# One row tile first: splitting the load and the norm of x ahead of a cross-attention loop

## The reference

```python
c = layernorm(x);  q = ctx
s = (c @ w_c + b_c)[:, :, None] + (q @ w_q + b_q)[:, None, :] + einsum('bcd,bqd,d->bcq', c, q, w_cq) + b_cq
a = softmax(s, axis=2);  c2q = a @ q
b = softmax(max(s, axis=2), axis=1);  q2c = b @ c
x = x + concat([c, c2q, c * c2q, c * q2c]) @ W_l.T + b_l
e = argmax(layernorm(x) @ wr + br)
x = x + gelu(layernorm(x) @ w1[e] + b1[e]) @ w2[e] + b2[e]
```

## Time and profile before

| | us |
|---|---|
| median of 3 runs | 275.74 |
| lowest, highest | 275.59, 278.57 |
| span of the profiled execution | 277.8 |
| the profiled execution's own time beyond its span | not listed |
| VectorE busy | 191.0 (69%) |
| ScalarE busy | 155.9 (56%) |
| GpSimd busy | 109.8 (40%) |

### The profile page before, as it was taken

The page is one execution under the profiler, slowest core; times in us unless marked ns, Lnnn a source line. Parts: engine busy times, 40 slices in busy tenths (PEclk is TensorE's granted clock), DMA queues, the critical chain, the costliest instruction groups (busy, mean ns, idle before and its releaser), DMA issues.

```text
span 277.8 us, 5155 instructions
## 1 busy us (share of the span) xinstructions
PE 202.6 (73%) x1661; PEld 143.8 (52%) x1662; DVE 191.0 (69%) x404; ACT 155.9 (56%) x244; POOL 109.8 (40%) x88
## 2 busy tenths in 40 slices
PE   0249489799779979899898995899540039788960
PEld 0113136556546756576566664799440029566850
DVE  2996967948967979889799798978643013465360
ACT  3299176695568569599595994891100016445430
POOL 2369991942901603507116069400004600424233
PEclk9999978979959999999999999899855556999797
DMA  6992079969968999999989989498001261111000
GB/s 252 391 347 79 0 229 179 250 135 204 249 165 153 226 236 228 247 226 252 255 211 261 235 198 214 113 227 146 0 0 38 104 182 48 43 29 43 10 22 0
DMA packets 129245, 44.64 MB, mean 161 GB/s; under 512 B 107927, under 2 KB 127023, under 8 KB 129231
## 3 DMA queue, kind: packets, MB, share of 16 engines
q1 hardware_dynamic: 128216, 42.87, 65.0%
q0 software_dynamic: 864, 1.58, 1.7%
q10 hardware_dynamic: 150, 0.00, 0.0%
HBM read 14.15 MB, written 4.01 MB: 65 GB/s over the span
## 4 chain that ended last, share of the span: by engine, by line
PE 40%; DVE 21%; issue 19%; ACT 8%; DMA 6%; POOL 3%; ACTq 1%; DVEq 0%; POOLq 0%
ACT Pf L564 5%; DVE S L702 5%; PE psS L922 5%; PE psO L937 4%; PE psS L923 4%; PE psS L924 4%; PE psX L937 4%; DVE Phl L720 3%; DMA PT<-Phl 3%; POOL rows_by_expert L502 2%; PE psS L1111 2%; PE psO L940 2%; DVE qTl L691 2%; DVE c_sb L666 2%; PE psX L940 2%
## 5 line engine op out<-in xcount | busy, mean ns | idle before, releaser
L702 DVE TENSOR_SCALAR_CACHE_REDUCE S<-psS 128x1024 f32<-128x1024 f32 (+1 forms) x56 | 61.8, 1105 | 23.7 <-PE psS L924 15.2
L564 ACT ACTIVATE Pf<-S,negb 128x1024 f32<-128x1024 f32 (+1 forms) x56 | 59.1, 1055 | 33.6 <-DVE negb L711 33.6
L720 DVE TENSOR_TENSOR Phl<-Pf,Phl 128x1024 f16<-128x1024 f32 x41 | 58.8, 1433 | 1.3 <-ACT Phl L580 1.3
L922 PE MATMUL psS<-qTh,gh 128*128 128x512 f16 (+1 forms) x104 | 42.0, 404 | 22.5 <-DVE S L702 9.3
L580 ACT CAST Phl<-Pf 128x1024 f16<-128x1024 f32 x48 | 50.2, 1046 | 10.1 <-DMA PT<-Phl 8.0
L447 POOL TENSOR_TENSOR Phl<-Pf,Phl 128x1024 f16<-128x1024 f32 x7 | 15.6, 2226 | 75.8 <-ACT Phl L580 75.8
L923 PE MATMUL psS<-qTl,gh 128*128 128x512 f16 (+1 forms) x104 | 41.8, 402 | 0.0
L924 PE MATMUL psS<-qTh,gl 128*128 128x512 f16 (+1 forms) x104 | 41.7, 401 | 0.0
L937 PE MATMUL psO<-qn,PT 128*128 128x256 f16 x204 | 39.7, 287 | 0.0
L940 PE MATMUL psO<-qn,PT 128*128 128x128 f16 x204 | 37.8, 228 | 0.0
L937 PE MATMUL psX<-qn,PT 128*128 128x256 f16 x204 | 37.5, 278 | 0.0
(11 more groups left out here) (182 smaller groups left out, 394.5 us busy)
## 6 DMA issues: line engine op xcount, KB each, us to landing
stageT<-in_w SPq DMA_DIRECT2D x8, 512.0 KB, 4.4
stageT<-in_ctxT SPq DMA_DIRECT2D x6, 512.0 KB, 6.6
PT<-in_ctx SPq DMA_DIRECT2D x6, 512.0 KB, 6.8
rows_by_expert<-stageT SPq DMA_DIRECT2D x5, 385.5 KB, 3.5
S<-rows_by_expert SPq DMA_DIRECT2D x1, 967.5 KB, 5.5
S<-rows_by_expert SPq DMA_DIRECT2D x15, 64.0 KB, 1.8
PT<-Phl SPq DMA_TRANSPOSE x48, 3.9
Pf<-in_x SPq DMA_DIRECT2D x1, 512.0 KB, 4.0
```

Of the source, the lines that this page charges most:

```text
L564: nc.scalar.activation(Pf[:, e % 3, 0:b - a], S[:, a:b], ACT.Exp, bias=negb[:, bass.ds(t, 1)], accum_out=Lp[:, bass.ds(t * NG + e, 1)]).th ...
L702: nc.vector.tensor_scalar(out=S[:, a:b], in0=psS[n % 3][:, 0:b - a], scalar1=1.0 / GS, scalar2=None, op0=ALU.mult, op1=ALU.max, accum_out= ...
L720: nc.vector.tensor_tensor(lo, Pf[:, e % 3, 0:hi.shape[1]], hi, ALU.subtract).then_inc(low_done, 1)
L922: nc.tensor.matmul(dst, g_h, qTh[:, a:b], start=True, stop=False)
```

## The change

x is loaded in two parts, row tile 0 straight into `c_sb`, then behind the first ctxT load the other seven. Row tile 0 is normalised, transposed and split alone; tiles 1 to 3 and 4 to 7 follow (`C_GROUPS`), with their statistics, scales and `c_sb` in different places of VectorE's list: the `c_sb` of tiles 1 to 3 and their g among the readouts of tile 0, those of tiles 4 to 7 after the first `negb`. The pieces whose low part GpSimd makes are 0, 2, 4, each in two halves with a semaphore count for each. ScalarE makes four `qn` casts before the first exponential and the other three between the pieces of tile 0, followed by the two cT copies and the late g behind pieces 4 and 5. `row_terms` moves from step 0 to step 1, and the steps 1 and 6 stand outside the loop. GpSimd's list is otherwise as it was.

```diff
+    EARLY = 4
+        C_GROUPS = ((0, 1), (1, H), (H, T))
-        POOL_LOW = (0, 2, 5)
+        POOL_LOW = (0, 2, 4)
-            sp.dma_start(x_sb[:, :, :], x.rearrange("(t p) d -> p t d", p=P)).then_inc(x_landed, 16)
+            sp.dma_start(c_sb[:, 0, :], x[0:P, :]).then_inc(x_landed, 16)
...
+                if n == 0:
+                    sp.dma_start(c_sb[:, 1:T, :],
+                                 x[P:N, :].rearrange("(t p) d -> p t d", p=P)).then_inc(x_rest_landed, 16)
...
             for n in POOL_LOW:
-                a, b = cols(n, GR)
                 pool.wait_ge(qTh_ready, n + 1)
-                nc.gpsimd.tensor_tensor(qTl[:, a:b], stageT[:, a:b], qTh[:, a:b],
-                                        ALU.subtract).then_inc(qTl_pool_ready, 1)
+                for c in (2 * n, 2 * n + 1):
+                    a, b = cols(c, CH)
+                    nc.gpsimd.tensor_tensor(qTl[:, a:b], stageT[:, a:b], qTh[:, a:b],
+                                            ALU.subtract).then_inc(qTl_pool_ready, 1)
...
-            deviation(1, 0, H)
+            deviation(1, 0, 1)
...
-                    deviation(2, H, T)
+                    deviation(2, 1, T)
...
-            act.wait_ge(cT_in_psum, 2)
-            act.wait_ge(g_ready, 2)
-            for h in range(2):
+            def keep_cT(h):
+                act.wait_ge(cT_in_psum, h + 2)
                 nc.scalar.copy(cT[:, h * CH:(h + 1) * CH], cT_psum[h][:, :]).then_inc(cT_ready, 1)
...
+            for n in range(EARLY):
+                high_qn(n)
...
-            step(0, False)
+            for e in range(NG):
+                exp_piece(0, e)
+                high(0, e, False)
+                if EARLY + e < NG:
+                    high_qn(EARLY + e)
+                elif e == EARLY:
+                    keep_cT(0)
+                elif e == EARLY + 1:
+                    keep_cT(1)
+                    late_g()
...
+            def first_g(k):
+                t0, t1 = C_GROUPS[k]
+                a, b = t0 * P, t1 * P
+                dve.wait_ge(cT_in_psum, k + 1)
+                link(nc.vector.tensor_scalar(g32[:, a:b], cT_psum[0][:, a:b], vecs16[:, 0:1], vecs16[:, 1:2],
+                                             ALU.mult, ALU.add))
+                link(nc.vector.tensor_copy(gh[:, a:b], g32[:, a:b]))
+                nc.vector.tensor_tensor(gl[:, a:b], g32[:, a:b], gh[:, a:b], ALU.subtract).then_inc(g_ready, 1)
...
+            dve.wait_ge(x_landed, 16)
+            statistics(c_sb, 0, 1)
+            normalise(c_sb, c_sb, 0, 1, c_ready)
+            dve.wait_ge(x_rest_landed, 16)
+            moments(c_sb, 1, H)
+            first_g(0)
+            link(moments(c_sb, H, T))
+            for t in range(1, T):
+                last = nc.vector.bn_aggr(out=mv[:, t, :], in_=st[:, t, :])
+            link(last)
+            variances(1, T)
...
+            low_qT(1)
+            scores(0, 0, False)
+            low_qT(3)
+            scores(0, 1, False)
+            scales(1, T)
+            standardise(c_sb, c_sb, 1, H, c_ready)
+            low_qT(5)
+            scores(0, 2, False)
+            low_qT(6)
+            scores(0, 3, False)
+            first_g(1)
+            for n in range(4, NG):
+                scores(0, n, False)
             row_max(0)
+            standardise(c_sb, c_sb, H, T, c_ready)
             step(0, 0, False, True)
-            dve.wait_ge(row_term_in_psum, 1)
-            nc.vector.tensor_copy(row_term[:, :], psX[:, 0:T]).then_inc(row_term_ready, 1)
-            with dve.Fori(1, T - 2, 2) as t:
-                step(t, 1, True, True)
-                step(t + 1, 0, True, True)
+            step(1, 1, True, True)
+            with dve.Fori(2, T - 2, 2) as t:
+                step(t, 0, True, True)
+                step(t + 1, 1, True, True)
+            step(T - 2, 0, True, True)
...
             def step(t, odd, has_prev, has_next):
                 for e in range(NG):
+                    if not has_prev and e == 2:
+                        turn_c(2)
                     if not has_prev and e == LAG:
+                        pe.wait_ge(cT_ready, 1)
+                    if isinstance(t, int) and t == 1 and e == 1:
                         row_terms()
+                    if isinstance(t, int) and t == 1 and e == LAG:
+                        pe.wait_ge(row_term_ready, 1)
...
+            pe.wait_ge(g_ready, 1)
+            for c in range(NCH):
...
+                if c == 5:
+                    turn_c(1)
             pe.wait_ge(g_ready, 2)
```

More of the change, by code:

```diff
@@ L337, in _ @@
             sp.wait_ge(qTl_ready, len(DVE_LOW))
[L338 removed]
+            sp.wait_ge(qTl_pool_ready, 2 * len(POOL_LOW))
             def load_w1(k):
@@ L535, in _, with high_qn @@
                 nc.scalar.copy(qTh[:, a:b], stageT[:, a:b]).then_inc(qTh_ready, 1)
-            for n in range(NG):
+            def high_qn(n):
                 act.wait_ge(qn_landed[n], 16)
@@ L642, in _, with moments, statistics @@
             norms = [0]
-            def statistics(src, t0, t1):
+            def moments(src, t0, t1):
                 for t in range(t0, t1):
                     last = nc.vector.bn_stats(out=st[:, t, :], in_=src[:, t, :])
-                link(last)
+                return last
+            def statistics(src, t0, t1):
+                link(moments(src, t0, t1))
                 for t in range(t0, t1):
@@ L651, in statistics, with variances, scales @@
                 link(last)
-            def normalise(src, dst, t0, t1, done):
+            def variances(t0, t1):
                 r = slice(t0, t1)
                 nc.vector.tensor_scalar(sc2[:, r], mv[:, r, 1], EPS, None, ALU.add).then_inc(var_ready, 1)
+            def scales(t0, t1):
+                r = slice(t0, t1)
                 norms[0] += 1
@@ L664, in normalise, with standardise @@
                 link(nc.vector.tensor_tensor(rstd[:, r], rstd[:, r], sc1[:, r], ALU.mult))
+            def standardise(src, dst, t0, t1, done):
                 for t in range(t0, t1):
@@ L667, in normalise @@
                                             ALU.subtract, ALU.mult).then_inc(done, 1)
-            dve.wait_ge(x_landed, 16)
-            statistics(x_sb, 0, H)
-            normalise(x_sb, c_sb, 0, H, c_ready)
+            def normalise(src, dst, t0, t1, done):
+                variances(t0, t1)
+                scales(t0, t1)
+                standardise(src, dst, t0, t1, done)
+            def first_g(k):
[6 more added lines that the diff above has]
+                nc.vector.tensor_tensor(gl[:, a:b], g32[:, a:b], gh[:, a:b], ALU.subtract).then_inc(g_ready, 1)
             dve.wait_ge(small_landed, 16 * NSMALL)
             nc.vector.tensor_scalar(vecs16[:, :], vecs[:, 0:2], GS, None, ALU.mult).then_inc(vecs16_ready, 1)
+            nc.vector.tensor_copy(b3r[:, :], b3s[:, :].broadcast_to([3, T])).then_inc(b3r_ready, 1)
             dve.wait_ge(vecs16_ready, 1)
[L675 to L682, removed]
-            statistics(x_sb, H, T)
-            normalise(x_sb, c_sb, H, T, c_ready)
+            dve.wait_ge(x_landed, 16)
[9 more added lines that the diff above has]
+            variances(1, T)
             def low_qT(n):
@@ L736, in step @@
                 for e in range(NG):
+                    if isinstance(t, int) and t == 1 and e == 1:
+                        dve.wait_ge(row_term_in_psum, 1)
+                        nc.vector.tensor_copy(row_term[:, :], psX[:, 0:T]).then_inc(row_term_ready, 1)
                     if e == LAG and has_prev:
@@ L899, in _, with turn_c @@
             pe.wait_ge(consts_ready, 3)
-            def turn_c(h):
-                for t in range(h * H, (h + 1) * H):
+            def turn_c(k):
+                for t in range(C_GROUPS[k][0], C_GROUPS[k][1]):
                     pe.wait_ge(c_ready, t + 1)
-                    last = nc.tensor.transpose(cT_psum[h][:, (t - h * H) * P:(t - h * H + 1) * P], c_sb[:, t, :],
+                    last = nc.tensor.transpose(cT_psum[t // H][:, (t % H) * P:(t % H + 1) * P], c_sb[:, t, :],
                                                idf[:, :])
```

44 lines of the change are left out of this document (20 added, 24 removed).

## The result

The changed kernel takes 287.0 us (median of 4, 286.54 to 287.85) where the kernel before takes 275.66 (median of 4, 272.67 to 278.57): ratio 1.0453, 95% interval 1.0365 to 1.054. The change is slower, as forecast. The forecast was 283.6, so the loss on the medians is 11.3 us where 7.9 was worked out; 287.0 lies inside the stated 279 to 289, but above the 281 to 286 of "my own case". On the two traces the loss is 285.1 - 277.8 = 7.3.

What follows compares the result with a forecast made beforehand. No engine is full; waits between engines bound the kernel, through when each row tile gets its softmax offset negb. Terms -2.6 + 9.5 + 1.0 = +7.9 us on the 275.74 median gave 283.6, range 279 to 289.

Steps and rivals of the forecast that it cites:

- (a): Start, loads: row tile 0 lands at 2.6 to 4.8 us, the small vectors at 4.0, the rest of x at 5.8.
- (b): Start, row tile 0 normalised alone: the first score matmul moves from 13.14 to 9.05 us, 4.1 earlier.
- (c): Start, VectorE's next statistics, aggregates and variance end at 10.85 us; the third ctxT cast follows at 11.2.
- (d): VectorE until the first negb: 15.8 us work plus 7.0 waiting for GpSimd, offset 0 near 33.8, 2.6 gained.
- (e): Tile 0, ScalarE: added casts and copies and a later transposing DMA put the late gh 19.7 us after negb.
- (f): Tile 0, GpSimd's unchanged order: low piece (0, 3) follows late gl and constants; seventh exponential 26.7 after negb, 9.5 us lost.
- (g): Step 0, TensorE: its fifth group waits for the first cT copy, 15.9 us after negb, at no cost.
- (h): Step 1, row terms moved in and DMAs queued: 1.0 us lost, ends 2.5 lost and 2 gained.
- (i): Unrolling steps 1 and T-2: costed at nothing, with 1 us allowed if unrolled code had to be fetched.
- Given back: Rival: tiles 1 and 2 return up to 8.2 us of the delay, 272.3 us, faster; 6 in 100.
- Row tile 0 not early: Rival: small vectors or rest of x land late, the start gains nothing, 286.2 us; 10 in 100.
- The start lost too: Rival: GpSimd gets between every two VectorE instructions, offset 0 at 37.6, total 288.4 us; 17 in 100.

Runs made afterwards that it cites:

- e3: The changed kernel with the scales of row tiles 1 to 7 moved directly behind their variance, ahead of GpSimd's third ctxT piece: 287.43 us, ratio 1.0477 to the kernel before.
- e5: e1 plus one wait: GpSimd's seven qn low parts are held until VectorE has made g of row tiles 1 to 3: 277.41 us, ratio 1.0103.
- e1: The changed kernel with GpSimd making low piece (0, 3) ahead of its wait for the late gh: 281.75 us, ratio 1.0256 to the kernel before.
- e2: The kernel before with one added wait: GpSimd waits for the sixth high part of tile 0 ahead of its late gl: 282.28 us, ratio 1.0326.
- e6: e1 with ScalarE copying the first half of cT before its first exponential instead of behind piece 4: 278.18 us, ratio 1.0124 to the kernel before.
- e11: The kernel before, unedited, timed and profiled once more: 277.44 us (272.53 to 278.66, 10 runs), ratio 0.997 to the same kernel.
- e8: The kernel before with GpSimd's route constants first and its qn low parts held until VectorE's last low part of ctxT: 278.15 us, ratio 1.0103.
- e10: e9 with all seven qn casts before ScalarE's first exponential instead of four: 270.28 us, ratio 0.988 to the kernel before.
- e9: e5 and e6 together, route constants at GpSimd's start, and the last four c_sb before GpSimd's held run: 272.58 us, ratio 0.9932 to the kernel before.

## Why the forecast held, and where its size was off

- **(a) Right, early.** Small vectors at 2.96 (forecast 4.0), row tile 0 with them; but the rest of x at 6.92 (5.8), for which VectorE waited 1.48.
- **(b) Right.** First score matmul at 9.39 (9.05) where the earlier trace rows have 13.14. The early landing was spent on the late rest, and on the cast `gh`, 1.07 from 7.94 beside 0.36 for three times its width later on.
- **(c) Right.** The variances end at 10.9; the next low part starts at 10.84.
- **(d) The waits were mis-sized.** From 10.84 to 35.38 are 24.5 us. Waits, by rows: 1.0 in the low part at 13.32, 6.3 in the four scales (6.99 less 4 x 0.17), 1.75 in the three `c_sb` (2.61 less 0.86), 0.5 for TensorE: 9.6, where 7.0 was put; the work was 15.0, where 15.8 was put. The premise "where VectorE's instructions stand back to back it seems to keep its turn" is refuted: by e3's three `c_sb`, 6.28, and e5's four, 7.71. The row at 18.63 was one case, in which GpSimd came out of a wait only 0.06 us before, and was read as a rule. The Trainium skill, "SBUF — State Buffer", section "Who interferes with whom", has the two engines shut each other out for a whole instruction when VectorE's has two SBUF inputs or uses a two-port mode; the held rows here agree, down to operations of 128x7. The trace adds that inside GpSimd's unbroken runs they took turns, so that each small VectorE instruction paid a whole 2.09 us subtraction.
- **(e) Mis-sized by 1.5.** The late gh is written 18.2 after the offset (19.7). The transposing DMA of the first piece is issued 3.9 after it (39.32), not 6.6: GpSimd had ended four `qn` pieces and waited, so low piece 0 met none.
- **(f) Right, and shown from both sides** (e1, e2). Tile 0 took 28.3 (28.7), ScalarE's wait 8.36 (7.0): `gl` took 2.11 instead of 1.15 and one select 1.21 instead of 0.98, which made up for (e).
- **(g) Right under its condition.** TensorE waited 8.54 for the first cT copy, and behind the stall that cost nothing. The clause "if (f) were not there this would cost" is what e1 and e6 show, at 5.0 us of tile 0. The stall hid this wait: taking the stall out gave 3.9 us of tile 0, and taking the wait out after it another 5.0.
- **(h) Not confirmed.** Tile 1 took 22.3 and 23.9 in the two profiles, before 22.9 and 23.0: between 0.6 gained and 1.0 lost. The wait for the row terms is there (2.49), but its price can't be told from that of the granted clock, 0.89 and 0.82 in these two.
- **(i)** Tile 6 of before and after take 18.3 and 18.2. No price of unrolling shows.
- **The missing 3.4 us, open.** Each run of after lies 1.7 to 1.8 above its span, so the span of 277.8 belongs to some 279.6, and the profiled execution of before was 3.9 above the median on which the sum was put. In the ten executions of e11 the kernel before took 272.53 at a granted clock of 0.924 and 278.66 at 0.896, and both its profiles are of long ones. On the trace the sum was +7.9 against +7.3 measured: 1.7 too much gain at offset 0, 0.4 too much loss in (f) and 1.6 in (h), and, in no step, 2.6 and 0.7 gained in tile 2 and at the end against 3.1 lost in tiles 3 and 4. That the two totals come so close is luck: these errors cancel, and the largest that stand in no step, 2.6 and 2.1, go with the granted clock. The prediction read the excess of tiles 1 and 2 over 17.8 without their clock, 0.89 and 0.88. On the median the sum was 3.4 short, and e2, which has the stall alone, is short in the same way. No trace shows where a short execution of before saves its 3.9 us, so the cause of this part stays open.
- **Rivals.** Given back: refuted by e2. Row tile 0 not early: refuted by (a), (b). The start lost too: offset 0 didn't go to 37.6, but net of the spread its gain is nil, where the forecast had 2.6, and by the total this rival (288.4) lay nearer to 287.0 than the forecast (283.6). Its mechanism, GpSimd between every two instructions that it can hold, is what the rows of the scales show.
- **Its bounds.** The lower one, 279.5, takes 0.5 off for (h), whose own best end was 2 gained; with that it would be 278.0. Nothing hung on it.

**What it would have taken.** Out of GpSimd's way, the early row tile 0 brings offset 0 to 26.95 (e5), where the kernel before has 36.27 and 34.34, and 33.35 with its own hold (e8): 6.4 to 9.3 us earlier. To have this in the total took GpSimd's `qn` subtractions out of the way, the low piece ahead of the late `gl`, the first cT copy in time, and all `c_sb` before GpSimd's run: each reordered an instruction list, none changed the work, and together with the casts of e10 they turn 287.0 into 270.3, on another chip (4.5% above the kernel before into 1.2% below it).

## What to carry to other kernels

When a step is moved later on one engine, go through every in-order list that waits for it, and look at what is queued behind that wait though it has nothing to do with it: here a 512-column cast, moved behind six exponentials, made the seventh wait 8.4 us through a GpSimd order that the change had left alone, and about 5 of them stood in the total. A stretch in which GpSimd subtracts in SBUF without a pause is the wrong place for many small VectorE operations with two SBUF inputs, or tensor_scalars from SBUF to SBUF, whatever their size. Moving them one place only hands the wait on (e3); move GpSimd's run, or the operations wholly out of it (e5, e9). And put a sum worked out on one profiled execution against that execution's own time, not against a median from which it may be 1.4% away.

## What the runs showed of the hardware

- Operations of 128x7 with two SBUF inputs (L691, L693), and a tensor_scalar with one (L692), took 2.04 to 2.05 us instead of 0.17, while a reciprocal of 128x7 started inside one of GpSimd's subtractions took 0.19. In e3 three 128x128 tensor_scalars took 6.28 and in e5 four took 7.71.
- The wait is felt in both directions: GpSimd's `gl`, 1.15 us in the earlier trace rows, took 2.11, and a select of 128x64 that takes 0.29 in e1 took 1.21.
- Tiles of the same work differ by up to 2.6 us with the granted clock between two offsets: tile 4 of after took 19.9 at 0.91, tile 5 took 17.8 at 1.00, and tile 2 took 20.9 at 0.88 before and 18.4 at 1.00 after.
